# Messages of a graph layer's edges: two VectorE operations a round, on four chunks each, in place of four on two

## The reference, cut to what matters

```python
h = (x @ W).reshape(N, H, C)                    # H = 8 heads, C = 32
alpha = leaky_relu(a_src[src] + a_dst[dst], 0.2)
ex = exp(alpha - amax[dst])
denom = segment_sum(ex, dst)
attn = ex / (denom[dst] + 1e-16)
msg = h[src] * attn[:, :, None]
out = segment_sum(msg, dst)
```

## Time and profile before

| | us |
|---|---|
| median of the three runs | 2732.33 |
| lowest and highest run | 2727.21, 2732.99 |
| profiled execution, span from first to last instruction | 3414.5 |
| stage of graph 1's edges in the profiled execution | 175 to 1562 |

### The profile page before, as it was taken

How to read it: one execution, slowest core, us unless ns; L and a number is a source line. 1 busy time by engine, 2 the same in 40 slices (tenths; PEclk the granted TensorE clock), 3 DMA queues, 4 the chain that set the end, 5 groups by cost and what they waited for, 6 DMA issues and landing times.

```text
span 3414.5 us, 41541 instructions
## 1 busy us (share of the span) xinstructions
PE 2388.5 (70%) x11358; PEld 1456.9 (43%) x11358; DVE 2070.0 (61%) x5801; ACT 899.5 (26%) x2266; POOL 1808.7 (53%) x2002
## 2 busy tenths in 40 slices
PE   3676776888888888877747666666666766666655
PEld 2443444545554554544534333333333334333334
DVE  7577887878878888878813443434443443333457
ACT  6411111222222222214613222222222222222213
POOL 0556676656656666665552554555555545455510
PEclk9778987999988999978768887877777777777777
DMA  4334444434434444351012112112221111111147
GB/s 148 118 88 112 112 113 117 105 96 102 111 96 109 103 108 105 101 146 63 7 41 61 43 46 51 41 46 44 44 57 43 44 46 40 38 46 38 44 147 263
DMA packets 171472, 280.05 MB, mean 82 GB/s; under 512 B 46278, under 2 KB 88836, under 8 KB 171236
## 3 DMA queue, kind: packets, MB, share of 16 engines
q0 software_dynamic: 69312, 133.61, 17.9%
q1 hardware_dynamic: 101924, 143.67, 12.9%
HBM read 236.30 MB, written 40.84 MB: 81 GB/s over the span
## 4 chain that ended last, share of the span: by engine, by line
PE 34%; DVE 23%; another core or an unknown queue 20%; issue 13%; DVEq 3%; ACT 2%; POOL 2%; ACTq 1%; DMA 1%; SPq 0%
PE pb L1283 7%; PE pb L1201 7%; PE pb L1187 5%; PE pb L1172 5%; DVE x_sb L2187 2%; DVE acc L2326 2%; PE pb L1164 2%; DVE big L1520 1%; DVEq L2320 1%; PE pb L1296 1%; PE pb L1079 1%; ACTq L830 1%; DVE x_sb L1774 1%; PE pb L1270 1%
## 5 line engine op out<-in xcount | busy, mean ns | idle before, releaser
L731 POOL DMA_INDIRECT Gb<-table,idx x592 | 606.0, 1024 | 369.3 <-PE pb L1283 159.9
L1187 PE MATMUL pb<-big,early 128*128 128x512 f32 (+1 forms) x832 | 528.8, 742 | 187.8 <-ACT Gb L819 100.7
L1201 PE MATMUL pb<-early,Gb 128*128 128x256 f32 x1568 | 492.7, 464 | 117.8 <-issue 83.3
L2254 DVE TENSOR_TENSOR idx<-pb,b2B 128x256 f32<-128x256 f32 x196 | 83.1, 424 | 774.1 <-remote 475.9
L1283 PE MATMUL pb<-Gb,Sall 128*128 128x264 f32 x1184 | 414.0, 453 | 49.4 <-DVE big L1520 27.2
L665 POOL DMA_INDIRECT dl<-table,idx x288 | 276.1, 959 | 314.6 <-DVE tmr L2309 134.2
L1201 PEld LDWEIGHTS pb<-early,Gb 128*128 128x128 f32 x1568 | 345.8, 233 | 222.7 <-issue 130.4
L2187 DVE TENSOR_SCALAR x_sb<-iota,x_sb 128x576 bf16<-128x576 f16 x1024 | 402.0, 432 | 0.3 <-PE pb L1173 0.3
L665 POOL DMA_INDIRECT tab<-table,idx x272 | 267.1, 982 | 237.6 <-DVE iota L2309 82.0
L731 POOL DMA_INDIRECT early<-table,idx x288 | 290.2, 1008 | 171.7 <-PE pb L1283 78.2
L1172 PE MATMUL pb<-x_sb 128*128 128x512 bf16 x1024 | 368.5, 401 | 6.9 <-DVE x_sb L2187 3.7
(11 more groups left out here) (427 smaller groups left out, 3670.5 us busy)
## 6 DMA issues: line engine op xcount, KB each, us to landing
Sall<-dlT SPq DMA_DIRECT2D x214, 256.0 KB
Y<-idx SPq DMA_DIRECT2D x96, 256.0 KB
big<-Y SPq DMA_DIRECT2D x16, 1024.0 KB, 11.0
x_sb<-in_x_dram SPq DMA_DIRECT2D x8, 1536.0 KB
Gb<-table,idx POOLq DMA_INDIRECT x592
early<-table,idx POOLq DMA_INDIRECT x560
out_dram<-x_sb SPq DMA_DIRECT2D x24, 256.0 KB
dl<-table,idx POOLq DMA_INDIRECT x288
```

Of the source, the lines that this page charges most:

```text
L731: g.indirect_dma_start(out=G1[i % 3][:, k, :], out_offset=None, in_=g1.table, in_offset=bass.IndirectOffsetOnAxis(ap=g1.idx[:, c:c + 1], a ...
L1187: t = pe.matmul(pbank[b][:, 0:nt * 128], W1s[:, w, k, f * 128:f * 128 + 128], xT[:, t0:t0 + nt, k * 128:k * 128 + 128], start=k == 0, stop ...
L1201: t = pe.matmul(pbank[b][:, 0:D], hh[:, bi % 2, f, j * 128:j * 128 + 128], W2s[:, w, f, :], start=f == 0, stop=f == 3)
```

## The change

The messages of a round are made by two operations on four chunks each (1024 elements a partition), at slots 4 and 6; before, there were four on two chunks each (512 elements), at slots 4 to 7. TensorE waits for them at every fourth chunk, and the counts of the semaphore go with it.

```diff
@@ tensor_program
                 for k in range(CG):
                     c = (i - 2) * CG + k
                     if c >= 0:
-                        if k % 2 == 0:
-                            pe.wait_ge(v_msg, 4 * (i - 2) + k // 2 + 1)
+                        if k % 4 == 0:
+                            pe.wait_ge(v_msg, 2 * (i - 2) + k // 4 + 1)
                         if k == 0:
                             pe.wait_ge(a_w32, i - 1)
@@ vector_program
             def messages(e, h):

-                o = slice(2 * h, 2 * h + 2)
+                o = slice(4 * h, 4 * h + 4)
                 hv = G1[e % 3][:, o, 0:256].rearrange("p c (h k) -> p c h k", k=32)
                 if h == 0:
                     v.wait_ge(a_ex, e + 1)
-                v.tensor_tensor(hv, hv, G1[e % 3][:, o, 256:264].unsqueeze(3).broadcast_to([128, 2, 8, 32]), ALU.mult).then_inc(v_msg, 1)
+                v.tensor_tensor(hv, hv, G1[e % 3][:, o, 256:264].unsqueeze(3).broadcast_to([128, 4, 8, 32]), ALU.mult).then_inc(v_msg, 1)
@@ the loop of vector_program
-                        if k >= 4:
-                            messages(i - 1, k - 4)
+                        if k in (4, 6):
+                            messages(i - 1, k // 2 - 2)
```

## The result

The changed kernel takes 2743.02 us in the median of four runs (2741.76 to 2747.33), against 2729.77 us for the kernel before: a ratio of 1.0053, with a 95% interval from 1.0038 to 1.0067. It is slower by 13.3 us in the medians and by some 14 us by the ratio; the forecast was 2742 us, in a range from 2714 to 2770.

A forecast was written before the change was run, and what follows sets the result against it. VectorE was taken to set the round, TensorE close behind and GpSimd's gather queue just under; longer holds on gathers outweighed VectorE's saving, +10 us on 2732.33, giving 2742 us, range 2714 to 2770.

The forecast's parts named there:

- the unexplained share of the chain: Waits on another core or unknown queue, 20.2% of the profile, 690 us, taken as time the timed runs mostly lack.
- VectorE's saving: Message operations on VectorE: 220 longer ones replace 440, saving 12.5 us in all, 31 at most.
- The coarser wait and lateness: TensorE waiting for four chunks costs 2 us, 5 at most; sums of slots 5 and 7 start about 0.5 us later.
- The gathers: GpSimd's row gathers, held under longer VectorE message operations: queue's round grows from 10.6 to 11.05 us, 53 us in all.
- the fourth gather: A gather starting together with a message operation takes 0.94 us, read as fitting the hold until 0.12 us before its end.
- The sum: Stage total: first stretch +8 us, second -4, third +4, coarser wait +2, together +10 us.
- the 0.48 us: Growth of the gather queue's need per round; half felt in the first stretch, +8 us.
- the 7 us: VectorE's gain in the second stretch, 0.11 us a round; the queue lets half pass, -4 us.
- B: Rival: the gather queue has room left, so VectorE's saving makes the kernel faster, 2720 to 2701 us; chance 0.25.
- C: Rival: gather queue bounds all 110 rounds, at the score's wait for gathers; 29 to 53 us slower, 2761 to 2785; chance 0.15.
- the lead at the start: Three rounds of gathers are fetched ahead; the first starts 32 us before the stage.
- D: Rival: TensorE sets the rounds and both effects stay below it, 2732 us, give or take 5; chance 0.15.

The follow-up runs named there:

- run 2: Kernel before, its two-chunk message operations kept, with only TensorE's wait made coarser, for two operations at once: ratio 0.9998.
- run 3: Kernel before with its two-chunk message operations moved to slots 4 and 6, two in each, and TensorE's wait left fine: ratio 1.0026.
- run 6: Kernel before with four-chunk operations in rounds 0 to 34 and 101 to 109 alone, two chunks in the middle rounds: ratio 1.0031.
- run 5: Kernel before with four-chunk operations in rounds 35 to 100 alone, two chunks in the others: ratio 1.0001.
- run 8: Changed kernel with messages reading the exponentials from PSUM, where ScalarE writes them as well; TensorE's next transposes wait for the messages: ratio 0.9963.
- run 4: Kernel before with eight message operations of one chunk each a round, two back to back in each slot: ratio 1.0084.

## Why the prediction was right, point by point

**What bounds the kernel.** Right in the main: VectorE and TensorE close to full with the gather queue just below. The estimate of the timed stage, 1187 us, came out at 1195.2, with rounds of 11.0 us; the way to it (take the unexplained share of the chain off the profiled span) held to 0.7% over the stage, but not for its parts: the first 34 rounds were put at 377 us and take 370.1, the next 68 at 728 and take 754.1. The queue's need was put at 10.6 us a round (10.0 + 0.54 is 10.54) and is 10.8: in the disturbed profile fewer gathers had a message operation in flight 0.1 us after their start (197, not 294).

**VectorE's saving.** 57 ns for each pair by start to start, not 140 by recorded lengths. The traces have 2 x 0.602 - 1.135 = 69 ns (medians from a message operation's start to the next start on VectorE), and VectorE is busy for 12.6 us less. Taking the overlap from two lines of the timeline was what kept this term small; by the recorded lengths it would have been 31 us, and the forecast a faster kernel.

**The coarser wait and lateness.** Costed at 2 us; run 2 shows none, within 2.7 us. In the changed kernel TensorE's waits for messages fell, from 17.1 us in 14 to 4.1 us in 2, and those for sums from 59.6 to 52.3 us. That the places have an effect of their own (run 3) I had not seen; it goes with longer gathers in the middle rounds.

**The gathers.** The mechanism was right, and so was its law for a gather that starts inside the operation (held to 0.12 us before its end). The reading of the fourth gather was not: one that starts with the operation and takes 0.94 us does not fit that law, which would give it 0.61 us more. Gathers that start within 0.05 us of it mostly go free (6 of 8 in the kernel before, 4 of 4 in the changed one), while six that start 0.15 to 0.20 us ahead of it are held through the whole of it in the changed kernel, up to 2.195 us.

The size of the term was not right either: I had 53 us more on the queue and the mean at 1.07 to 1.08 us. The mean is 1.082, but the growth is 0.034 x 880 = 30 us, from a higher start: a gather took 1.048 - 0.945 = 0.103 us more than an unheld one in the kernel before, where the first profile had 0.073. Summed over the gathers that had a message operation in flight 0.1 us after their start, the holds are 62 us before and 82 us after, so 0.14 and 0.37 us for an operation; I had worked out 0.126 and 0.49. The gathers do not start evenly over the long operation, as I had assumed: of 199, 29 start 0.25 to 0.30 us after it and 83 start 0.85 to 0.90. Another 8 us of the growth are gathers that start 0.1 to 0.2 us ahead of a message operation (1 us before, 9 after), and the last 3 lie elsewhere. That 0.50 us a round agreed with the 0.54 read from the first profile was luck: of the 65 us of extra gather time there, only 40 belong to message operations. That the queue then sets the round came true at 11.1 us, where the sum had 11.05.

**The sum.** +10 was forecast, +13.3 measured. That 2742 us lies within 1 us of the measured time is luck in part: it is counted from 2732.33 us, and the kernel before came out at 2729.77 with its fourth run. Two errors offset each other in the sum: the queue's growth was put too high and its start too low. The halves in it (half of the 0.48 us is felt, half of the 7 us passes) came from no row. Of the stretches, the ends lost as said in direction (+12 forecast, 8.5 us both in run 6 and in the two profiles). The middle was to gain 4 us; it lost 4.3 us in the profile of the changed kernel and came out at nothing, within 2.7 us, in run 5. There the part of the queue was too small in the sum.

**The rivals.** B, the queue has room, was wrong for the changed kernel but describes what happens once the holds are gone (run 8, 0.9963). C would have needed 29 us, but its place is largely what the traces show: the score waits for gathers, and the queue's need meets the round in the first 35 rounds (11.02 of 11.03 us) and in the middle 66 (11.15 of 11.17). Its price was too large because the lead at the start does help (880 gathers need 1221 us by their mean and their gaps, and the stage takes 1208.2) and the stage before was 8 us longer than the estimate. D is excluded by the interval, whose lower end is 10 us above no change.

What stays open: why the first 35 rounds, where VectorE is busy for only 90% of the time, lose with shorter operations too (run 4); why other gathers than those under the messages grew in run 3; what the holds cost with two chunks, for which there is no control; and whether short operations spread with gaps between them would lower the holds, which wasn't tried.

## What to carry to other kernels

An operation of VectorE that reads two tensors in SBUF, as the messages do here, can stop GpSimd's indirect gathers for nearly as long as it lasts; before making it longer look at how full the gather queue is, and consider reading one operand from PSUM. Check with the trace which gathers grew: in run 3 the mean rose, but not through the operations that had been moved. Count an operation's cost on a full engine from start to start of consecutive lines, not by its recorded length. And when a profile is much longer than the timed runs, take a second one before resting a size on it.

## What the runs showed of the hardware that I had not expected

What decides how long a gather is held is where it starts, within a twentieth of a microsecond. Of two message operations back to back, the second kept waiting 14 of the 16 gathers that started 0.15 to 0.20 us after the first (1.92 us in the median), and one of the 36 that started 0.20 to 0.55 us after it (run 3). A gather that starts 0.15 to 0.20 us ahead of a long operation can be held through the whole of it (2.19 us, six of ten in the changed kernel), one that starts with it mostly goes free. And a broadcast operand in PSUM costs VectorE nothing over one in SBUF at this size: 1.209 against 1.216 us in the median for 1024 float32 elements, with the next operation starting 1.13 us after either.
